# Softmax denominators as columns, their reciprocals spread over the heads' rows by TensorE, in a four-layer attention and expert kernel

## What is computed

```python
# layers 0 and 1: heads of 64 (16 heads in layer 0, 8 in layer 1)
attn = softmax(q @ k.T / 8)          # layer 0 clips q @ k.T / 8 to -11..11; layer 1 also attends to its own 512 rows
out  = attn @ v                      # per head, 512 queries of each of 2 batches
y    = out.reshape(512, heads * 64) @ Wo
# layers 2 and 3: 16 heads of 16 (layer 2 causal over 512 keys, layer 3 over 1024 keys, with rotary embedding)
attn = softmax(q @ k.T / 4)
out  = attn @ v
y    = out.reshape(512, 256) @ Wo
```

## Time and profile before

| | |
|---|---|
| median of 3 runs | 2956.81 us (2956.66 to 2959.81) |
| profiled execution | 2951.47 us, span of the profile 2949.7 us |
| attention, layer 0 / 1 / 2 / 3 | from about 30 to 620, 960 to 1384, 1590 to 1866, 2128 to 2553 us |
| experts behind them | the rest |
| reciprocals of 128x512 | 24 of L824 and 16 of L1381 |

### The profile page before, as it was taken

How to read it: one execution, slowest core, us unless ns; L and a number is a source line. 1 busy time by engine, 2 the same in 40 slices (tenths; PEclk the granted TensorE clock), 3 DMA queues, 4 the chain that set the end, 5 groups by cost and what they waited for, 6 DMA issues and landing times.

```text
span 2949.7 us, 31683 instructions
## 1 busy us (share of the span) xinstructions
PE 2375.2 (81%) x11832; PEld 1668.5 (57%) x11832; DVE 1576.8 (53%) x2705; ACT 907.5 (31%) x1752; POOL 948.3 (32%) x817
## 2 busy tenths in 40 slices
PE   3799999848968999996885777399788989659994
PEld 2455555528955555553874454289644444348884
DVE  5788888743145665653315766322477767421222
ACT  2454555412124444442112223000224444401111
POOL 2354554433332342333222211355400000044443
PEclk8899999959978999997897777599879999769997
DMA  3000000008930000000482321199522221048883
GB/s 119 1 9 10 18 10 10 1 33 310 316 128 1 0 10 9 1 1 15 157 273 71 80 65 50 48 318 327 164 57 69 59 62 45 17 170 298 300 296 116
DMA packets 103178, 298.08 MB, mean 101 GB/s; under 512 B 16913, under 2 KB 45841, under 8 KB 102641
## 3 DMA queue, kind: packets, MB, share of 16 engines
q0 software_dynamic: 45168, 206.99, 20.3%
q1 hardware_dynamic: 57856, 89.07, 10.2%
HBM read 244.22 MB, written 20.32 MB: 90 GB/s over the span
## 4 chain that ended last, share of the span: by engine, by line
PE 41%; DVE 12%; issue 7%; DMA 4%; POOL 2%; ACT 2%; SPq 0%; another core or an unknown queue 0%; DVEq 0%; POOLq 0%; ACTq 0%
PE psum L1860 8%; PE psum L275 7%; PE psum L1883 6%; PE psum L1211 3%; DVE plain L1363 3%; PE psum L1224 2%; PE psum L646 2%; DMA plain<-in_l_en,plain 2%; PE psum L1184 2%; PE psum L661 2%; DVE plain L1381 2%; DMA plain<-sorted_x 2%; DVE plain L1360 1%; PE psum L1250 1%; PE psum L664 1%
## 5 line engine op out<-in xcount | busy, mean ns | idle before, releaser
L275 PE MATMUL psum<-split 128*128 128x512 f32 (+1 forms) x1776 | 475.3, 416 | 57.1 <-DVE split L348 11.1
L1860 PE MATMUL psum<-plain 128*128 128x128 f32 x3904 | 494.4, 279 | 10.2 <-DMA plain<-in_l_shared 8.5
L1860 PEld LDWEIGHTS psum<-plain 128*128 128x128 f32 x3904 | 486.3, 196 | 22.3 <-issue 10.5
L275 PEld LDWEIGHTS psum<-split 128*128 128x128 f32 x1776 | 337.0, 208 | 191.8 <-issue 95.7
L1009 POOL TENSOR_TENSOR plain<-plain 128x1024 f32<-128x1024 f32 x144 | 363.5, 2524 | 239.8 <-DVE plain L807 195.9
L1984 POOL DMA_INDIRECT plain<-in_l_ffn,plain x274 | 259.8, 948 | 401.7 <-PE psum L1883 378.7
L948 ACT ACTIVATE plain<-psum 128x512 f32<-128x512 f32 x448 | 251.4, 595 | 310.5 <-PE psum L664 145.2
L1883 PE MATMUL psum<-plain 128*128 128x256 f32 x1160 | 304.2, 385 | 28.0 <-DVE plain L1949 25.5
L1480 ACT ACTIVATE plain<-psum 128x512 f32<-128x512 f32 (+3 forms) x384 | 185.8, 542 | 228.7 <-PE psum L1224 227.6
L646 PE MATMUL psum<-plain 128*64 128x512 f32 x896 | 236.9, 616 | 5.6 <-DVE plain L814 5.6
L1949 DVE TENSOR_TENSOR plain<-plain,psum 128x256 f32<-128x256 f32 x198 | 81.7, 419 | 298.2 <-ACT plain L1908 266.5
(11 more groups left out here) (177 smaller groups left out, 3024.7 us busy)
## 6 DMA issues: line engine op xcount, KB each, us to landing
split<-split SPq DMA_DIRECT2D x288, 64.0 KB, 2.0
split<-split SPq DMA_DIRECT2D x96, 128.0 KB, 2.4
plain<-sorted_x SPq DMA_DIRECT2D x76, 128.0 KB
sorted_y<-plain SPq DMA_DIRECT2D x76, 128.0 KB
plain<-in_l_w SPq DMA_DIRECT2D x16, 512.0 KB
plain<-in_l_w SPq DMA_DIRECT2D x12, 640.0 KB, 3.8
plain<-in_l_ffn,plain POOLq DMA_INDIRECT x274
plain<-in_ctx SPq DMA_DIRECT2D x8, 512.0 KB, 6.1
```

What stands on the lines that cost most here:

```text
L275: m = t.e.matmul(out, lhs[x], rhs[y], start=(first and n == 0), stop=(last and n == 2), skip_group_check=skip)
L1860: m = t.e.matmul(K.bank(b)[:, 256 * z + P * f:256 * z + P * f + P], ws[:, f, c0:c0 + 128], xt[:, k, :], start=(f == 0 and k == 0 and z == ...
```

## The change

The denominators are computed with the queries on the partitions. In layers 0 and 1, for each quarter q of 128 queries and each head h, a 128x128 piece of `SA` is the stationary operand and one column of ones moves through; eight matmuls leave the denominators in 8 columns of a bank. In layers 2 and 3 a 128x128 piece of `OU` is stationary and 4 columns of `SEL` move; four matmuls leave 16 columns. VectorE takes the reciprocal of these 8 or 16 columns into `RCP`. A new piece of side work, `spread`, brings them back: for each quarter and head, one column of `RCP`, broadcast to 64 (or 32) columns, is stationary and the identity moves through, which writes the 128 reciprocals of that quarter on all of the head's rows. VectorE multiplies by the bank. In layers 0 and 1 ScalarE now copies bank 4 to `OT` first (one more ACTIVATE a step), so that the product reads PSUM only once, and this copy frees bank 4 (`heads_copied64`).

```diff
+        self.RCP = small(16)
...
-        total = sum(prep) + 1.5
+        total = sum(prep) + 1.7
-            weights = [0.5] * (n > 0) + ahead[:2] + [1.0] * (n > 0) + ahead[2:]
+            weights = [0.4] * (n > 0) + [0.3] * (n > 0) + ahead[:2] + [1.0] * (n > 0) + ahead[2:]
...
-def side64(n, A, divide, prepare, output, tail):
+def side64(n, A, divide, spread, prepare, output, tail):
     if n:
         divide(n - 1)
+        yield
+        spread(n - 1)
         yield
...
 # TensorE, layers 0 and 1
         weigh(n, nk - 1)
+        t.emptied(4, "heads_copied64")
     def divide(n):
-        for h in range(2):
-            m = t.e.matmul(K.bank(b)[64 * h:64 * h + 64, :], K.ONES, A.SA[n % 2][:, h, :], start=True, stop=True)
+        for q in range(4):
+            for h in range(2):
+                m = t.e.matmul(K.bank(b)[:, 2 * q + h:2 * q + h + 1], A.SA[n % 2][:, h, 128 * q:128 * q + 128],
+                               K.ONES[:, 0:1], start=True, stop=True)
         t.emptied(b, "recip")
-        t.emptied(4, "divided")
+    def spread(n):
+        b = RB.get()
+        t.bank(b)
+        t.wait_ge("recip", t.made["sums"])
+        for q in range(4):
+            for h in range(2):
+                m = t.e.matmul(K.bank(b)[64 * h:64 * h + 64, 128 * q:128 * q + 128],
+                               K.RCP[:, 2 * q + h:2 * q + h + 1].to_broadcast([P, 64]), K.ID, start=True, stop=True)
+        m.then_inc(*t.up("spread"))
+        t.emptied(b, "divided")
...
 # VectorE, layers 0 and 1
-        v.e.reciprocal(A.OT, K.where("sums", k)).then_inc(*v.up("recip"))
-        v.e.tensor_tensor(A.OT, K.bank(4), A.OT, ALU.mult).then_inc(*v.up("divided"))
+        v.e.reciprocal(K.RCP[:, 0:8], K.where("sums", k)[:, 0:8]).then_inc(*v.up("recip"))
+    def spread(n):
+        v.wait_ge("heads_copied64", bases["heads_copied64"] + n + 1)
+        v.wait_ge("spread", k)
+        v.e.tensor_tensor(A.OT, A.OT, K.where("spread", k), ALU.mult).then_inc(*v.up("divided"))
...
 # ScalarE, layers 0 and 1
+    def divide(n):
+        s.wait_ge("weighed", wv0 + nk * (n + 1))
+        s.wait_ge("out", bases["out"] + 4 * n)
+        s.e.activation(A.OT, K.bank(4), ACT.Copy).then_inc(*s.up("heads_copied64"))
...
 # layers 2 and 3
-            weights = [1.0] + [1.0] * (i > 0)
+            weights = [0.8] + [0.6] * (i > 0) + [0.6] * (i > 0)
-        t.e.matmul(K.bank(b), A.SEL, A.OU, start=True, stop=True).then_inc(*t.up("sums", L, n))
+        for q in range(4):
+            m = t.e.matmul(K.bank(b)[:, 4 * q:4 * q + 4], A.OU[:, 128 * q:128 * q + 128],
+                           A.SEL.rearrange("p (j c) -> p j c", c=32)[:, :, 0], start=True, stop=True)
+    def spread(n):
+        t.wait_ge("recip", (L, n))
+        for q in range(4):
+            for j in range(4):
+                m = t.e.matmul(K.bank(b)[32 * j:32 * j + 32, 128 * q:128 * q + 128],
+                               K.RCP[:, 4 * q + j:4 * q + j + 1].to_broadcast([P, 32]), K.ID, start=True, stop=True)
-        v.e.reciprocal(A.RC, K.bank(K.at.get(("sums", L, n), 0))).then_inc(*v.up("recip", L, n))
-        v.e.tensor_tensor(A.OU, A.OU, A.RC, ALU.mult).then_inc(*v.up("divided", L, n))
+        v.e.reciprocal(K.RCP, K.bank(K.at.get(("sums", L, n), 0))[:, 0:16]).then_inc(*v.up("recip", L, n))
+        v.e.tensor_tensor(A.OU, A.OU, K.bank(K.at.get(("spread", L, n), 0)), ALU.mult).then_inc(*v.up("divided", L, n))
```

More of the change, by code:

```diff
@@ L704, in tensor_attention64 @@
     for n in range(A.n):
-        side = side64(n, A, divide, prepare, output, tail)
+        side = side64(n, A, divide, spread, prepare, output, tail)
         attend(n, side)
@@ L708, in tensor_attention64 @@
     divide(n)
+    spread(n)
     output(n)
@@ L713, in vector_attention64 @@
     own, nk = A.own, A.nk
-    wv0, ex0, o0 = (bases[x] for x in ("weighed", "exp", "out"))
+    wv0, ex0 = bases["weighed"], bases["exp"]
     v.next("biased", 0 if own else 8)
@@ L961, in scalar_attention64 @@
     for n in range(A.n):
-        side = side64(n, A, nothing, prepare, nothing, tail)
+        side = side64(n, A, divide, nothing, prepare, nothing, tail)
         attend(n, side)
         run(side, 1000)
+    divide(n)
 def gpsimd_attention64(g, K, A, bases):
@@ L1032, in gpsimd_attention64 @@
     for n in range(A.n):
-        side = side64(n, A, nothing, prepare, nothing, tail)
+        side = side64(n, A, nothing, nothing, prepare, nothing, tail)
         attend(n, side)
@@ L1094, in tm, with side16 @@
         return self.TM[(n * self.rows + c) % 2]
-def side16(n, A, place, wsplit, divide, values_weight, rowmax, output, load_out, shift, proj, tail):
+def side16(n, A, place, wsplit, divide, spread, values_weight, rowmax, output, load_out, shift, proj, tail):
     ahead = n + 1 < A.n
@@ L1264, in tensor_attention16 @@
             project_values(A.steps[n][0])
-        side = side16(n, A, nothing, nothing, divide, nothing, rowmax, output, nothing, shift, proj, tail)
+        side = side16(n, A, nothing, nothing, divide, spread, nothing, rowmax, output, nothing, shift, proj, tail)
         attend(n, side)
@@ L1379, in divide, with spread @@
         v.wait_ge("sums", (L, n))
[L1380 to L1383 removed]
+        if n:
+            v.wait_ge("spread", (L, n - 1))
+        v.e.reciprocal(K.RCP, K.bank(K.at.get(("sums", L, n), 0))[:, 0:16]).then_inc(*v.up("recip", L, n))
+    def spread(n):
+        v.wait_ge("spread", (L, n))
+        v.e.tensor_tensor(A.OU, A.OU, K.bank(K.at.get(("spread", L, n), 0)), ALU.mult).then_inc(*v.up("divided", L, n))
     def output(n):
@@ L1532, in gpsimd_attention16 @@
     for n in range(A.n):
[L1533 removed]
+        side = side16(n, A, nothing, wsplit, nothing, nothing, nothing, rowmax, nothing, nothing, nothing, proj, tail)
         for kt in range(nk):
@@ L1606, in sync_attention16 @@
     for n in range(A.n):
-        run(side16(n, A, place, wsplit, nothing, values_weight, rowmax, nothing, load_out, shift, nothing, nothing),
+        run(side16(n, A, place, wsplit, nothing, nothing, values_weight, rowmax, nothing, load_out, shift, nothing, nothing),
             1000)
```

17 lines of the change are left out of this document (10 added, 7 removed).

## The result

| | before | after |
|---|---|---|
| median, runs taken side by side | 2958.31 us (2956.66 to 2961.71, 4 runs) | 3018.07 us (3012.99 to 3025.6, 4 runs) |
| ratio, 95% interval | | 1.0212 [1.0192, 1.0231] |
| profiled execution, its span | 2951.47 us, 2949.7 us | 3012.99 us, 3011.3 us |
| mean granted clock of the whole span | 0.883 | 0.875 |

What follows compares the result with a forecast made beforehand. TensorE was taken as the path in layers 0 and 1, VectorE only in layers 2, 3 and the ends. 33 + 19 - 2 + 4 + 1 = +55 us gave 3012 us; 2972 to 3045 held eight in ten.

Steps and rivals of the forecast that it cites:

- What bounds the kernel: TensorE is the path in layers 0 and 1; VectorE's 126 us gain counts only in layers 2, 3 and layer ends.
- The term of a step in layer 0, +2.2 us: Middle of layer 0: sums 1.69, round trip 0.5, spread 1.0, less 1.01 removed; times 15 steps, +33 us.
- The lower bound of the step, +1.1: Smallest net cost given for a middle step of layer 0; the upper bound was +3.3 us.
- the rival of cheap one-column sums: Sums at 0.05 us each if moving columns counted and the load hid: -25 us, total 2987; 12%.
- its first rival: The clock falls in layer 0 too: 23 to 38 us more over 15 steps, total about 3040; 20%.
- weight loads keep coming: The reason given against a fall of the clock in layer 0, the rival held at 20%.
- the 0.95 that the prediction named as a sign of being wrong: A granted clock under 0.95 in layer 0 would show the forecast wrong and the falling-clock rival true.
- The 0.5 us wait: TensorE's round trip between sums and spread for the short reciprocal, 0.5 us, bounds 0.4 and 0.7.
- Layer 1, +19 us: Middle of layer 1: three steps at +2.2 us and four, with some half clock, at +3.2.
- Nothing pays it back: Middle of layer 0: VectorE's earlier finish wins no time, as the 1.44 us gap before L661 recurs.
- Layers 2 and 3, -2 and +4 us: Middle steps, seven per layer: layer 3 -0.3 us a step, -2 us; layer 2 +0.6 a step, +4 us.
- The four ends, +1 us: Layer ends, where nothing lies beside the denominators: zero in layer 3, about +0.7 us each in layers 0 and 1.

Runs made afterwards that it cites:

- cols64: The changed kernel with 64 columns of ones moving through each sum of layers 0 and 1 instead of one; 2978.17 us in one run.
- widesums: The changed kernel with the old wide matmuls for the sums of layers 0 and 1, short reciprocal and spread kept, product not the softmax; 2950.38 us, one run.
- behind: The changed kernel with the next step's first projection put ahead of the sums in layers 0 and 1; 2976.69 us in one run.
- copy64: The kernel before with the reciprocal of layers 0 and 1 replaced by a copy of the bank, output not divided; 2939.61 us, ratio 0.9925.
- apart: The changed kernel with the next step's first projection put between sums and spread in layers 0 and 1; 3014.94 us in one run.
- copy16: The kernel before with the reciprocal of layers 2 and 3 replaced by a copy of the bank, output not divided; 2936.57 us, ratio 0.993.

## Why the prediction was right, and where it was wrong

The time, 3018 us, lies 6 us above the forecast of 3012 and inside the range, and the direction and its reason were right. That it is so close is luck: layers 0 and 1 cost 38 us more than forecast (26.6 and 11.6), and layers 2 and 3 and the stretches between cost 32 us less (8.9, 11.5 and 11.3).

- **What bounds the kernel: right.** VectorE lost 124 us of work and the kernel got slower, since TensorE is the path in layers 0 and 1.
- **The term of a step in layer 0, +2.2 us: right at full clock.** Sums 1.84, wait 0.39, spread 1.03 us against 1.69, 0.5 and 1.0; `cols64` gives +30 us for layer 0 and +19 for layer 1, against +33 and +19, though its +30 holds two falls of the clock and the gain in the last step. The lower bound of the step, +1.1, should be +1.0 by its own parts (0.8 + 0.4 + 0.8 - 1.01). That the weight load sets the spacing, taken from L1738, was right; the rival of cheap one-column sums falls.
- **The clock of layer 0: the forecast failed, its first rival came true.** I gave 20% to a fall of the clock, against it "weight loads keep coming". The clock of 0.92 is below the 0.95 that the prediction named as a sign of being wrong. The middle steps take 35.3 to 36.9 us instead of 34.1, and layer 0 takes 29.6 us more than in `cols64`, within the 23 to 38 forecast for the rival; only the rival's total, 3025 to 3055, was too high, for what came back elsewhere. `cols64`, `widesums` and `behind` show that in this layer it took one-column sums and the gap close ahead of them. The 0.5 us wait that I named beside them has no part that could be seen.
- **Layer 1, +19 us: too low by 12.** I took 1.0 us more in four of seven steps. Sums, wait and spread at half clock cost 5.6 us instead of 3.2, so a step that falls pays 2.4, 6 us more than forecast in four steps. The low clock also lasts beyond them, over the projection and the next scores:

```profile
1091.00:1100.00 9.00, 8.70 (x41) 7.53 (x41) 0.90 (x2) 1.68 (x3) 0.00 (x0) 0.50 0.00 0
```

  From the first to the last sums the granted clock is 0.93 of 431.5 us where it was 0.97 of 400.9, which makes some 60 us at half clock instead of some 20. What those cost beyond the sums and the spread had no term in the forecast.
- **"Nothing pays it back": wrong.** `copy64` puts VectorE's relief at 7.7 + 8.3 = 16 us in layers 0 and 1. I had looked at the middle steps only, where it is some 0.3 us in layer 0; about half is in each layer's last step, where the output waits for the product.
- **Layers 2 and 3, -2 and +4 us: sign of the second wrong, size of both.** The failing term is the spread, "32 instructions at 0.06, between 0.05 and 0.07": it is 0.032, so 1.0 us instead of 1.9. My bound came from L1211 with 32-column loads but 256 moving columns, another form. From the first sum to the third row maximum layer 3 now takes 3.51 us (2345.46 to 2348.97) instead of the forecast's 4.2 and the 4.55 before, so 1.0 us a step or 7 in all. The rest of its 13.5 is, by subtraction, the clock's, which I hadn't counted: the falls behind the six stalls are gone and the layer rose from 0.94 to 1.00. In layer 2 the same stretch is 5.37 us in the first step, at half clock, and 4.73 in the second, against 5.9 forecast and 5.36 before.
- **The four ends, +1 us: nearly right, sign apart.** From the last sum to the output: layer 0 6.17 to 6.63 us, layer 3 6.09 to 4.89. The rows of layer 3's end after:

```profile
2602.74 1.71 PE L1272 MATMUL psum<-plain 128*128 128x4 f32 x8
2604.89 1.94 PE L1285 MATMUL psum<-plain 128*32 128x128 f32 x32 [0.44 <-DVE plain L1430]
2607.63 3.78 PE L1297 MATMUL psum<-plain 128*128 128x256 f32 x8 [0.80 <-DVE plain L1434]
```

- **Open.** Why the stretches from layer 1 to 2 and from 2 to 3 are shorter with the new denominators, and what of layer 2's gain is spread and what is clock. Why the clock held with wider moving columns isn't shown either, only that it fell in 2 of 14 middle steps instead of in all; `cols64`, `widesums`, `apart` and `behind` are one run each, and it is the repetition from step to step within each run that carries the reading.

## What to carry to other kernels

Swapping a wide operation of a relieved engine for small matmuls pays where TensorE stood waiting (layers 2 and 3, -24 us) and not where it was the path (+85 us): make such a change layer by layer. When matmuls are small, count weight loads, and try more moving columns: here 64 instead of one cost 0.16 us a step, and the clock fell far less often. Before calling a relief worthless, look at the last step of each loop, where nothing lies beside it, and see what a faster operation will then run into on the memory that it shares.

## What the runs showed of the hardware

- Sixteen float32 instructions with 128-column weight loads take 1.84 us with 1 moving column and 2.00 with 64; at half clock 3.40.
- With 128 moving columns, 32-column loads in four column groups come 0.032 us apart, 64-column loads in two groups 0.064. Whether the load's width or the groups' overlap sets this isn't told apart.
- One-column sums about 1.2 us behind a 1.44 us gap brought the granted clock down in all fourteen middle steps of layer 0; the same with 64 columns in 2 of 14, and one-column sums with a projection of 1.4 us between gap and sums in none of the thirteen steps of the window.
- VectorE's reciprocal of float32 in PSUM took 3.36 us for 128x512, 0.26 for 128x16, 0.21 for 128x8; a copy of 128x512 took 0.69.
- VectorE's product with both operands in SBUF took 2.0 to 2.9 us when it started during a GpSimd product of 2.36 (8 of 8 in `copy16`); with one in PSUM always 0.69 (10 such in the changed kernel).
